# A decoder layer's wide attention loop: probability-value products in batches of four steps, row sums one step sooner

## The reference, cut to what matters

```python
probs = softmax(q k^T / sqrt(16) * mod)           # 16 heads of 16: "narrow"
ctx = probs v
causal = mha(x, x, ca_Win, ca_Wout, 4 heads)      # 4 heads of 64: "wide", attention c
ctx = ctx * (1 - 0.7) + causal * 0.7              # "joint" work
meta = mha(ctx, ctx, mc_Win, mc_Wout, 4 heads)    # 4 heads of 64: "wide", attention m
ctx = ctx * (1 - META_W) + meta * META_W          # "norm" work
x1 = layernorm(x + ctx @ Wo + bo)
```

## Time and profile before

| | us |
|---|---|
| median of 3 runs | 3048.09 |
| lowest, highest | 3040.52, 3054.56 |
| profiled execution | 3030.39 |
| its span, first to last instruction | 3028.6 |
| TensorE busy | 2765.4 (91%) |
| VectorE busy | 2019.9 (67%) |
| ScalarE busy | 1424.6 (47%) |
| GpSimd busy | 980.7 (32%) |
| mean granted TensorE clock | 0.961 of full speed |

### The profile page before, as it was taken

One profiled execution on the slowest core, in us unless ns is written; L12 is line 12 of the kernel. 1 busy time (PEld: TensorE's weight loads), 2 busy tenths in 40 slices (PEclk: granted clock), 3 DMA queues, 4 the chain that ended last, 5 costly groups with the idle time before them and its releaser, 6 DMA issues. The chain is left out here.

```text
span 3028.6 us, 42693 instructions
## 1 busy us (share of the span) xinstructions
PE 2765.4 (91%) x14144; PEld 1787.5 (59%) x14145; DVE 2019.9 (67%) x3033; ACT 1424.6 (47%) x2556; POOL 980.7 (32%) x1000
## 2 busy tenths in 40 slices
PE   7989999999999889999998999868998679999995
PEld 6754545555545345555555555446666459888895
DVE  4568777777777298887887888555665557333337
ACT  2315666666666634444443544433444343233334
POOL 4457530000000044343345555453000360343322
PEclk9979999999999999999999999978999899999998
DMA  6999985353533155555555453345665433323425
GB/s 219 316 257 271 243 225 76 49 75 50 78 46 47 28 126 144 156 163 157 146 155 150 127 139 98 103 134 97 114 109 92 128 103 113 134 78 111 174 84 167
DMA packets 246189, 400.00 MB, mean 132 GB/s; under 512 B 37711, under 2 KB 147895, under 8 KB 244727
## 3 DMA queue, kind: packets, MB, share of 16 engines
q1 hardware_dynamic: 177940, 251.20, 31.4%
q10 hardware_dynamic: 49299, 82.70, 12.9%
q0 software_dynamic: 18768, 63.79, 6.7%
HBM read 231.46 MB, written 166.14 MB: 131 GB/s over the span
## 5 line engine op out<-in xcount | busy, mean ns | idle before, releaser
L654 DVE TENSOR_REDUCE an_m<-an_psm 128x1 f32<-128x1024 f32 x512 | 595.4, 1217 | 181.6 <-PE an_psm L578 181.5
L635 ACT ACTIVATE an_probs<-an_pst 128x512 f32<-128x512 f32 x1024 | 539.8, 605 | 304.4 <-PE an_pst L608 299.7
L1409 ACT ACTIVATE wj_probs<-wj_pst 128x512 f32<-128x512 f32 x512 | 297.7, 595 | 347.4 <-PE wj_pst L1251 338.6
L1126 POOL TENSOR_TENSOR wj_sums<-wj_sums,wj_probs 128x512 f32<-128x512 f32 x192 | 267.6, 1394 | 312.7 <-ACT wj_probs L1409 309.6
L1440 DVE TENSOR_REDUCE wj_m<-wj_pm 128x1 f32<-128x512 f32 x512 | 324.0, 679 | 17.4 <-PE wj_pm L1226 16.8
L1240 PE MATMUL wj_pacc<-wj_probs,wj_vs 128*64 128x512 f32 x1024 | 249.4, 608 | 2.8 <-ACT wj_probs L1409 2.8
L578 PE MATMUL an_psm<-an_ks,an_qs 127*128 127x512 f32 x640 | 224.5, 432 | 6.2 <-DVE an_m L654 6.2
L608 PE MATMUL an_pst<-an_qs,an_ks 128*128 128x512 f32 x640 | 209.7, 404 | 8.1 <-ACT an_probs L635 7.0
L1166 POOL MEMSET wj_qs<- 64x2048 f32 x2 | 3.5, 1800 | 620.1 <-issue 620.1
L1251 PE MATMUL wj_pst<-wj_qs,wj_ks 128*128 128x512 f32 x512 | 203.7, 398 | 0.0
L1126 DVE TENSOR_TENSOR wj_sums<-wj_sums,wj_probs 128x512 f32<-128x512 f32 x192 | 179.4, 935 | 20.2 <-ACT wj_probs L1409 20.2
(11 more groups left out here) (431 smaller groups left out, 6009.4 us busy)
## 6 DMA issues: line engine op xcount, KB each, us to landing
ew_w<-scr_ws SPq DMA_DIRECT2D x10, 3072.0 KB, 12.0
scr_ws<-wide_pair POOLq DMA_DIRECT2D x27, 1024.0 KB, 5.6
ac_qs<-scr_xq ACTq DMA_DIRECT2D x48, 256.0 KB, 5.1
an_qs<-scr_q SPq DMA_DIRECT2D x40, 256.0 KB, 11.6
an_ks<-scr_k SPq DMA_DIRECT2D x40, 256.0 KB, 13.1
wj_qs<-scr_mq ACTq DMA_DIRECT2D x18, 512.0 KB, 5.1
wj_ks<-scr_mk ACTq DMA_DIRECT2D x18, 512.0 KB, 5.9
scr_xs<-x_acc SPq DMA_DIRECT2D x2, 4128.0 KB, 15.9
```

Source lines behind the costliest of these rows:

```text
L635: act.activation(probs[:, (NSTEP * G + s) % HELD, j], pst[:, (GH * s + j) % RING], ACT.Exp, scale=HD ** -0.5).then_inc(exp_done, 1)
L654: dve.tensor_reduce(m1[:, hq, col:col + 1], psm[:, n % 2], AX.XY, ALU.max).then_inc(mx_done, 1)
L1126: eng.tensor_tensor(sums[:, x % CPB, j], earlier, probs[:, s % RING, j], ALU.add).then_inc(sum_done[j], 1)
L1409: act.activation(probs[:, x % RING, j], pst[:, j], ACT.Exp, scale=BHD ** -0.5).then_inc(exp_done, 1)
```

## The change

`values` takes the first step of a batch of four and is called at each step x > 0 that is divisible by four, with the products of x-4 to x-1; it waits for the exponentials step by step inside the batch, no longer once for both. The last batch is issued at x = 256. The unit `attend sums` moves from step 8(x+1)+1 to 8(x+1), where it again comes directly behind a batch. All other units, their order among themselves and the waits of the other engines keep their form; since VectorE answers a unit one step after it, its copy of the row sums (L1467) moves one step sooner too.

```diff
-        LASTPAIR = STEPS // 2 - 1
+        BATCH = 4
...
         for x in range(BLOCKS):
-            work.setdefault(KC * (x + 1) + 1, []).insert(0, ("attend", "sums", x, 0))
+            work.setdefault(KC * (x + 1), []).insert(0, ("attend", "sums", x, 0))
...
-            def values(t):
-
-                pe.wait_ge(exp_done, HP * (2 * t + 2))
-                x, kc = divmod(2 * t, KC)
+            def values(first):
+
+                x, kc = divmod(first, KC)
                 slot = x // CPB % SLOT
                 if kc == 0 and x:
 
                     pe.wait_ge(acc_out, x)
-                for s in (2 * t, 2 * t + 1):
+                for s in range(first, first + BATCH):
                     kc = s % KC
+                    pe.wait_ge(exp_done, HP * (s + 1))
...
-                t = x // 2
-                if s % 2 == 1 and t:
-                    values(t - 1)
+                if x and x % BATCH == 0:
+                    values(x - BATCH)
...
                 elif x == STEPS:
-                    values(LASTPAIR)
+                    values(STEPS - BATCH)
```

## The result

The changed kernel takes 3096.24 us, median of four runs (3089.65 to 3107.31), against 3048.04 us (3040.52 to 3054.56) for the kernel before: ratio 1.0163, 95% interval 1.0124 to 1.0201. That is 48 us slower, where I had forecast 8, and above the range of 3028 to 3080 us. A second measurement, in another series, gave 1.0163 [1.0128, 1.0198].

What follows compares the result with a forecast made beforehand. TensorE's own work was taken to set the end. Terms -12.2 + 10.5 + 2 + 4 + 2 + 1.4 gave +7.7 us on the median 3048.09, so 3056 us, range 3028 to 3080: no change, leaning to slower.

Steps and rivals of the forecast that it cites:

- The batches: Value products on TensorE: 64 batches instead of 128 save an entry and exit of 0.19 us each, 12.2 us less.
- R4: Rival: the 0.19 us is paid inside the long batch, so only the stalls remain; 3055 to 3068 us, chance 0.08.
- I go through the steps ... where something is late: Placing: walk through a group's steps for late ScalarE and VectorE work that the long odd steps had covered.
- (a): Norm groups, steps 4 to 6: late exponentials on ScalarE, then VectorE's addition and corrections, stall TensorE; +1.2 us per group.
- (b): Norm groups, step 15: normalising behind GpSimd's chain stalls TensorE 3.6 us against 2.7; +0.9 us per group.
- (c): Joint groups, steps 15 to 6: late reciprocals delay selector products, +0.6 in even groups, -0.15 in odd; together +2 us.
- R3: Rival: half clock follows each of the five step 15 stalls, +8.5 us, so 3064 us; chance 0.10.
- (d): Groups 0 and 1: VectorE's reductions and additions overrun three bare steps by 0.25 to 0.9 us per batch; +4 us.
- R2: Rival: VectorE's backlog bounds, the maxima's wait on PSUM banks comes in most groups; 3075 to 3085 us, chance 0.15.
- R1: Rival: VectorE and ScalarE catch up during the 3.9 us batch, so the kernel gets faster; 3022 to 3030 us, chance 0.22.
- (e): Last group, without maxima, bare steps bound by exponentials: the stalls of norm steps 4 to 6 come again; +2 us.
- (f): Row sums one step sooner: in the first norm group the wait for GpSimd's late additions has less cover; +1.4 us.

Runs made afterwards that it cites:

- experiment 1: Changed kernel with GpSimd's correction for a mix moved ahead of its addition of the same step; ratio 1.0090 to the kernel before, loop 902 us.
- experiment 2: Changed kernel with ScalarE's normalising of a chunk done one step later; ratio 1.0114 to the kernel before, loop 907 us.
- experiment 5: Changed kernel with the row sums back at one step later, so batches of four alone; ratio 1.0138 to the kernel before, loop 910 us.
- experiment 3: Changed kernel with both repairs, GpSimd's correction ahead of its addition and normalising one step later; ratio 0.9993 to the kernel before, loop 874 us.

## Why the prediction was wrong

**The batches: right, and too small.** 64 batches of 16 records, entry and exit 0.32 and 0.34 us, as predicted. I had 3.74 us for a batch; at full clock it takes 3.59 from its start to the next (1851.89 to 1855.48 above). Against the 1.86 us of eight records, eight records more cost 1.73 us, 0.43 a pair and not 0.47. The starts of the single records show 0.43 between the inner pairs at both lengths, but 0.48 from the first pair to the second and 0.53 from the last pair to the next product. So 0.15 us of what a batch pays at its ends lies inside it; I had spread this over its four pairs. The ends cost 0.34 us in all instead of 0.19, and their saving is 64 x 0.34 = 21.8 us instead of 12.2. R4 is false.

**The step that failed: "I go through the steps ... where something is late", with its list (a), (b), (c).** I followed each unit to the engine that answers it, and on to the corrections on VectorE (`cnb`), but not to the correction of the mix on GpSimd, `zb` at L1204, though my own description of the glue names it. Step 9 is one of the "three steps of bare 1.41 us" that follow a batch, and I tested only steps 5, 6, 15 and 0 to 4 for what they had covered. The same walk on the trace of before would have given it. From the start of step 9: its first scores 0.47, two exponentials 1.07, a handover of 0.12, GpSimd's addition and its correction. The addition is the first of a block (two tiles of probabilities, no running sum), with a median of 1.74 us over 32 of them before, 1.65 after; the correction takes 1.29. That makes 4.7 us, against two bare steps of 1.41: a stall of 1.9. In group 13 it is 2.29; over 14 waits 32.0 us, and its removal gave 32 us of loop, 22 by the ratios (experiment 1).

**(a), norm steps 4 to 6.** The waits are where they were said to be: 0.73 us on the exponential ahead of step 5's end, 1.46 on `cnb` in step 6. TensorE and ScalarE, group 13:

```profile
1832.42 0.50 PE L1285 MATMUL wj_pg<-wj_rs,wj_sel 128*128 128x512 f32 x1 [0.90 <-DVE wj_zb L1504]
...
1843.02 0.50 PE L1249 MATMUL wj_pst<-wj_qs,wj_ks 128*128 128x512 f32 x1 [0.73 <-ACT wj_probs L1408]
...
1846.14 0.47 PE L50 MATMUL wj_pg<-wj_cna,wj_w 128*128 128x512 f32 x1 [1.46 <-DVE wj_cnb L1552]
```

By the step lengths, steps 5 and 6 take 8.3 us where they would take 5.6 without a wait: 2.7 a group, before 0.6, so +2.1 where I had +1.2. The first row is one that I hadn't: in step 3 the second selector product waits 0.90 us for VectorE to free its bank, which cost step 3 1.4 us (1.9 to 3.3).

**(b), step 15.** Right chain, sized too short: the stall is 4.40 us in four of the five groups and 4.12 in the fifth, where I had 3.6. Before it was 2.45 in four and 2.73 in one, and I had taken the row of that one. That is +1.8 a group instead of +0.9. The missing term stood in my own: ahead of its chain GpSimd waits 0.93 us for VectorE's statistics, and I added the addition (1.3) and the chain (5.3) without it. After, in group 14:

```profile
1936.31 0.23 POOL L1155 TENSOR_SCALAR wj_ve<-wj_mv 128x4 f32<-128x4 f32 x1 [0.93 <-DVE wj_mv L1512]
```

In the fifth group this wait is missing, but GpSimd's addition takes 1.82 us. The half clock behind the stall comes on top (1.6 to 2.8 us in step 0). Its removal gave 26 us of loop (experiment 2), 5.5 in a norm group, 15 us by the ratios.

**R3, the clock: dismissed wrongly.** I gave it 0.10, because the row with a 2.73 us stall showed full clock behind it. But the trace of before held nearer evidence against me that I left out, so the sentence that it agrees "for the long standstill only" is wrong. In three of the four odd joint groups the wait of step 13 was followed by 3.4 us at half clock, though it lasted only 1.77, 1.96 and 1.73 us. Of the kernel before, TensorE in group 3 and the windows behind it in groups 3 and 7:

```profile
1267.20 0.50 PE L1249 MATMUL wj_pst<-wide_pair 128*128 128x512 f32 x1 [1.77 <-ACT wj_probs L1409]
...
1269.00:1272.40 3.40, 3.40 (x15) 3.15 (x14) 3.40 (x7) 0.60 (x1) 1.28 (x2) 0.50 0.71 223
1490.90:1494.30 3.40, 3.40 (x13) 2.70 (x12) 3.40 (x6) 1.61 (x3) 1.84 (x2) 0.50 0.41 158
```

After the change, all five stalls of step 15 were followed by half clock, and so were nine of the fourteen waits of step 10, which are shorter than the 2.73 us of that row. 58 us more of half clock in the loop cost 8 to 20 us. What I priced at 8.5 us and gave a chance of 0.10 came true, in about this size or more. The Trainium skill, "TensorE: Matmul & The Clock Gate", section "Why this matters for your kernels", warns against idle gaps between bursts; for the stalls of 4.1 us and more the runs agree with it, and I had set my one shorter row above it.

**(c), joint groups.** Reciprocals are sent off 2.3 us into the group (I said 3.4) and the selector products' step 2 lasts 2.0 to 3.9 us; a small cost, as predicted. The odd groups' store wait vanished instead of shrinking by 0.5, because step 10 stood still first; in experiment 1 it is back. The +10 of the joint groups is the wait of step 10 (the step takes 5.4 to 6.6 us instead of 2.9), less what the batches save and what the vanished store wait gives back.

**(d) and R2, VectorE.** (d) was about right: the +0.6 us of groups 0 and 1 is net of their batches' saving of 8 x 0.34 = 2.7, so the placing cost some 3.3 us there against +4, and the wait of TensorE's loads for the maxima's banks in these two groups rose from 11.5 to 15.6 us. R2 is false: over the whole loop that wait fell from 28.3 to 22.4 us, and VectorE's load in the joint groups is 368 of 458 us, 80%. It catches up during the batch, as R1 had said for this engine.

**(e), the last group.** +9 instead of +2: it has the mix and so the wait of step 10 (5.1 us for the step, before 2.5), half clock at its start (step 0 7.8 us), and its step 6 lasts 6.9 us, before 3.9. Step 6 is the path of (a) again, but longer:

```profile
1971.48 0.77 PE L50 MATMUL wj_pg<-wj_cna,wj_w 128*128 128x512 f32 x1 [2.95 <-DVE wj_cnb L1552]
```

VectorE's two corrections took 3.43 us there, before 2.39, and the clock halves at 1969.2.

**(f), sooner row sums.** Booked at +1.4 with the argument that they stand behind a batch in either case. But they too move from the step that had to cover the correction into the step that delays it: 24 us of loop in the profiles of experiment 5, and 8 to 10 us by the times, which they can't tell from nothing. How much this term was off therefore stays open.

Summed by what was repaired: 32 us (step 10) and 26 us (step 15), clock included, are 58 of the 62 us of the profiles; by the times both repairs together bring back 52 us. The other 4 are what the repaired kernel has over the one before: the batches save about 22 us of it, so some 26 us are spent elsewhere. Step 11 of the norm groups (about 12 us, experiment 3) is the largest part that can be named; (a), the selector products, the start of the norm groups (step 0 7.4 us after the repair) and groups 10 and 15 can be seen in the step lengths. I haven't priced these one by one.

## What to carry to other kernels

When products are collected into fewer, longer batches, list for every step that becomes bare *all* instructions that must finish inside it, engine by engine in their program order, corrections and helpers included; a step is safe only if each chain fits. Where an engine runs small urgent work behind its routine work, put the urgent work first: one such reordering on GpSimd was worth 32 us of the loop here (22 by the times), as much as the batches or more. After such a repair look at the next step as well: behind the correction stood a second addition of GpSimd's, which then held TensorE. And a change that pays in one stage and loses in another can be limited to the stage where it pays.

## What the runs showed of the hardware

**Half clock behind short waits.** In six of the eight joint groups the wait of step 10 (some 2.3 us) was followed by 3.4 us at a granted clock of 0.50, so that step 11 lasted 3.1 to 4.0 us; in groups 4 and 9, with step 10 at 5.4 us, it wasn't, and step 11 lasted 2.8. The kernel before had half clock behind waits of 1.73 to 1.96 us in groups 3, 7 and 9, and none behind five stalls of 2.45 to 2.73 us (the longest is in the earlier trace rows). So the length of the wait alone doesn't decide it, and what else does stays open. Half clock costs 1.4 us in the batch alone (5.01 against 3.65 us) and up to 2.8 in step 0 (8.8 against 6.0). Idle products in the gaps took most of it away (75 us to 14 in one series, 78 to 24 in the other), but removing the gap takes away both.

**The ends of a batch.** Between 128-column products, a batch of 64-column fp32 products takes 0.43 us a pair, and at its ends 0.34 us more in all: 0.19 ahead of and behind it, 0.15 in its first and last pair. Both figures are the same for 8 and 16 records. Read from a batch of 8 records alone, 0.15 us of the ends looks like a slower pair (0.47 us).

**Additions of GpSimd and VectorE side by side.** In step 12 of the norm groups both engines add probabilities to their running sums, and one of the two is long. First VectorE in group 12 of the kernel before, to be read beside GpSimd's 1.29 us of the earlier trace rows, then VectorE in group 12 after, beside GpSimd's 1.82 us above:

```profile
1768.63 1.80 DVE L1126 TENSOR_TENSOR wj_sums<-wj_sums,wj_probs 128x512 f32<-128x512 f32 x1
```

```profile
1806.97 0.68 DVE L1126 TENSOR_TENSOR wj_sums<-wj_sums,wj_probs 128x512 f32<-128x512 f32 x1
```

Over groups 10 to 14 of both kernels there are only these two cases: GpSimd 1.27 to 1.29 and VectorE 1.57 to 1.80 us, once before and four times after; or GpSimd 1.81 to 1.84 and VectorE 0.68, four times before and once after. In the first case VectorE's statistics come late, and with them the chain of step 15: the longer stalls of both kernels (2.73 and 4.40) are those. The additions that open a block fit: in the kernel before, the 26 of GpSimd with over 0.4 us of VectorE's addition beside them took 1.57 to 1.79 us, the other six 1.27 to 1.29. It looks as if one addition is held up while the other runs; no experiment here moved them apart.
